# Placed orders by engine, W2 kept in SBUF, and a dense last batch in a block of linear attention and mixture of experts

## The chip, the cores and the metric

One NeuronCore of a Trainium2 chip. TensorE (PE) multiplies matrices, VectorE (DVE), ScalarE (ACT) and GpSimd (POOL) work on tiles, SyncE (SP) issues DMAs; ScalarE and GpSimd issue some too. The time is device microseconds of one execution, lower is better.

## The reference

Eight batches of 1024 tokens, width 128, float32. Each batch goes through attention and then through a mixture of experts, each behind a layer norm that is modulated by the batch's condition vector:

```python
h = _layernorm(x) * (1 + ca) + sa
x = x + ga * attn(h)          # q, k, v, gate = h @ W.T; 8 heads of 16
h = _layernorm(x) * (1 + cb) + sb
x = x + gb * ffn(h)
# attn: rope on q and k; kv = sum_s k v; ksum, vsum
#   o = (q kv / 4 + vsum) / (q ksum / 4 + S) + conv5(v);  return (o * gate) @ Wo.T
# ffn: gates = the two largest of 8 softmax probabilities, scaled to sum 1, else 0
#   y = sum_e gates[:, e] * (gelu(x @ W1[e] + b1[e]) @ W2[e] + b2[e])     # W1 128x256, W2 256x128
```

## The kernel before, in words

A batch is eight blocks of 128 tokens (`J`), handled in two halves of 512 (`CH`). Its attention part, in order: statistics on VectorE (`stat1`), the reciprocal root on GpSimd (`pow1`, L613), the norm on ScalarE (`app1`, L489), transposes to put channels on partitions (`xT`, L337), the q, k, v products of 384 columns a block (`qkv`, L347), rope on VectorE block by block (L777, L779, with the sum of two blocks in L782) and v's eviction on ScalarE (L514), the sums over tokens (`kv`, L360), the transposes of v and q (L354, L368), denominator (`den`, L375), numerator and the spread denominator (`dn`, L381, L386), gate (L391), output product (`out`, L400), the residual (L817), second statistics, `pow2`, `app2`, transposes (`x1T`, L407) and router logits (`logit`, L415).

The sort: VectorE finds the two experts of each token in a chain of small operations (`choose` from L684, `soften`), TensorE counts the ranks (`prefix`, L424 and L426), VectorE makes from them a row number for each token and choice (`put`; `slots`) and the expert of each of 23 tiles of 128 rows (`owner`). GpSimd then scatters the normed rows into `x_sort` in HBM by 16 indirect DMAs of 128 rows (`scat`, L637).

The experts run over the 23 tiles: SyncE reads the tile's expert from `owner` into a register and loads that expert's W1, W2 and b1 as one piece of 514 columns into a ring of eight `wbuf` (`w`, L288 and L289), and four tiles of rows at a time (`xg`). TensorE transposes four tiles (`xsT`, L439), ScalarE evicts them with the modulation (L564), TensorE runs the first layer for couples of tiles (`l1`, L451), ScalarE the gelu (L574), TensorE the second layer (`l2`, L462); ScalarE evicts (`oev`, L582) and issues the store to `o_sort` (`ost`, L590). When all are stored, GpSimd gathers two rows for each token by 16 indirect DMAs (`gat`, L647), VectorE adds them times their gates to the bias product (`comb`, L833 and L836; `b2`, L470), and finishes (`fin`, L842, L845). SyncE stores the output (L303). A float32 product runs as two passes, so it has two records; a transpose has one.

The order on every engine comes from one table: each step has a tick (`AT`), each batch an offset (`BEGIN` for attention and sort, `BEGIN_EXPERTS` for the rest), and all engines walk the steps of all batches in the order of the sum. Attention of batches starts about 162 ticks apart, and the experts of a batch come some 420 to 600 ticks after its first transposes, so the experts of batch b lie beside the attention of batch b + 3, and those of the last three batches beside none. Every engine executes in order, so a wait holds back all that stands behind it. Attention's products share three PSUM banks in turn (`BANKS`). x_sort has four buffers, o_sort two, x1 and the gates are kept for five batches (`LAG`). A batch's first store to `o_sort` waits for the combination of two batches before; its first gather for the batch before (`s_comb`).

## Time and profile before

| | |
|---|---|
| median of 3 runs | 648.53 us (645.81 to 649.82) |
| the profiled execution, first to last instruction | 656.4 us |
| TensorE, weight loads | 453.0 us (69%), 373.7 us (57%) |
| VectorE, ScalarE, GpSimd | 328.3, 298.8, 298.5 us |
| DMA | 107.81 MB, mean 164 GB/s |
| mean granted clock of TensorE | 0.827 |

The profile is one execution under the profiler. Its own time is the span in the second row, and it is about 1% above the runs. Busy times are those of records: a TensorE record says when an instruction was taken up, and its end is modelled. "Issue" or "remote" behind a wait means that no event in the profile explains it.

### The profile page before, as it was taken

The numbers are of one execution on the slowest core, as the hardware profiler recorded it, in microseconds if no ns is written. First come the engines' busy times: TensorE is split into PE (matmuls) and PEld (weight loads), VectorE is DVE, ScalarE is ACT, GpSimd is POOL, SyncE is SP. The second block draws the span as 40 slices with busy tenths as digits, with TensorE's granted clock in tenths as the row PEclk, the third lists the DMA queues.
The fourth block names the chain that finished last, engine by engine and source line by source line (L and its number), as shares of the span: only waits on it lengthen the run. The fifth ranks groups of instructions, "written<-read, shape, count | busy, mean of one in ns | idle before, by whom it ended". The sixth has DMA issues, their size and how long they took to land.

```text
span 656.4 us, 9883 instructions
## 1 busy us (share of the span) xinstructions
PE 453.0 (69%) x2808; PEld 373.7 (57%) x2808; DVE 328.3 (50%) x1070; ACT 298.8 (46%) x805; POOL 298.5 (45%) x293
## 2 busy tenths in 40 slices
PE   2887769699795898587947988398639116693710
PEld 1555439589584876485827976296528115682600
DVE  3678889387372766375743856294127000220242
ACT  1545438478571756265624846173513004361400
POOL 1112463532757275717472557445744760027053
PEclk9987699899987899779875899599955657896765
DMA  7704039688673867277645765566744325975422
GB/s 233 224 1 124 22 107 271 195 233 240 177 218 81 231 199 224 75 220 195 181 133 157 208 183 166 160 186 179 203 137 148 109 73 148 282 213 179 132 64 60
DMA packets 113845, 107.81 MB, mean 164 GB/s; under 512 B 10040, under 2 KB 85440, under 8 KB 113536
## 3 DMA queue, kind: packets, MB, share of 16 engines
q1 hardware_dynamic: 80848, 77.76, 41.8%
q0 software_dynamic: 8192, 16.79, 8.4%
q10 hardware_dynamic: 24752, 12.64, 6.5%
q8 instruction: 23, 0.38, 0.3%
q14 instruction: 30, 0.25, 0.1%
HBM read 76.47 MB, written 30.68 MB: 163 GB/s over the span
## 4 chain that ended last, share of the span: by engine, by line
PE 39%; another core or an unknown queue 23%; DVE 13%; ACT 9%; POOL 6%; issue 6%; DMA 3%; SPq 2%; ACTq 0%; POOLq 0%; DVEq 0%
PE ps_o L462 9%; PE ps_hid L451 9%; PE bank L347 5%; PE bank L360 3%; ACT xn L489 3%; ACT hid L574 2%; PE ps_x L439 2%; DVE stats L658 2%; POOL og L647 2%; POOL x_sort L637 2%; PE ps_z L470 2%; PE bank L415 1%; POOL rstd L613 1%; PE bank L400 1%
## 5 line engine op out<-in xcount | busy, mean ns | idle before, releaser
L637 POOL DMA_INDIRECT x_sort<-xn,slots x128 | 140.6, 1098 | 136.3 <-DVEq L742 100.7
L647 POOL DMA_INDIRECT og<-o_sort,slots x128 | 123.4, 964 | 111.0 <-DMA o_sort<-o_s 46.7
L574 ACT ACTIVATE hid<-ps_hid,wbuf 128x128 f32<-128x128 f32 x368 | 105.1, 377 | 121.3 <-remote 66.5
L462 PE MATMUL ps_o<-wbuf,hid 128*128 128x128 f32 x736 | 111.6, 302 | 65.5 <-issue 41.2
L462 PEld LDWEIGHTS ps_o<-wbuf,hid 128*128 128x128 f32 x736 | 101.1, 212 | 77.5 <-issue 48.2
L451 PE MATMUL ps_hid<-xs_t,wbuf 128*128 128x128 f32 x736 | 111.2, 296 | 14.9 <-issue 11.8
L451 PEld LDWEIGHTS ps_hid<-xs_t,wbuf 128*128 128x128 f32 x736 | 101.5, 210 | 25.1 <-issue 20.1
L833 DVE SCALAR_TENSOR_TENSOR u<-og,gate,ps_z 128x128 f32<-128x128 f32 x64 | 21.9, 343 | 125.4 <-PE ps_z L470 112.2
L613 POOL TENSOR_TENSOR rstd<-var_eps,minus_half 128x8 f32<-128x8 f32 x16 | 27.0, 1688 | 97.1 <-DVE var_eps L668 96.5
L347 PE MATMUL bank<-wqkvg_f,h 128*128 128x384 f32 x128 | 52.3, 531 | 8.9 <-ACT v L514 7.0
L564 ACT ACTIVATE xs_t<-ps_x,mod 128x512 f32<-128x512 f32 (+1 forms) x48 | 37.4, 779 | 24.2 <-PE ps_x L439 13.9
L760 DVE SCALAR_TENSOR_TENSOR conv<-v_t,lepe_f,conv 128x1024 f32<-128x1024 f32 x32 | 40.6, 1269 | 0.2
L777 DVE TENSOR_TENSOR qk_cos<-bank,rope_f 128x256 f32<-128x256 f32 x64 | 26.8, 419 | 27.5 <-PE bank L347 21.0
L582 ACT ACTIVATE o_s<-ps_o 128x512 f32<-128x512 f32 (+1 forms) x48 | 28.4, 592 | 25.8 <-remote 15.3
L347 PEld LDWEIGHTS bank<-wqkvg_f,h 128*128 128x128 f32 x128 | 22.9, 204 | 26.1 <-ACT v L514 14.1
L684 DVE TENSOR_TENSOR logit<-bank,br_f 128x64 f32<-128x64 f32 x8 | 1.8, 222 | 67.3 <-remote 60.8
L439 PE MATMUL ps_x<-consts_f,xg 128*128 128x128 f32 x184 | 30.9, 289 | 6.0 <-DMA xg<-x_sort 4.1
L360 PE MATMUL bank<-v,qk 128*128 128x129 f32 x128 | 22.8, 351 | 16.9 <-DVE logit L684 16.8
L514 ACT ACTIVATE v<-bank 128x128 f32<-128x128 f32 x64 | 16.5, 280 | 35.7 <-DVE qk_sin L779 32.6
L360 PEld LDWEIGHTS bank<-v,qk 128*128 128x128 f32 x128 | 21.8, 264 | 17.7 <-issue 17.5
L489 ACT ACTIVATE xn<-xs,shift,rstd 128x128 f32<-128x128 f32 x64 | 26.2, 507 | 9.7 <-POOL shift L615 9.7
L470 PE MATMUL ps_z<-b_f,gates_t 64*128 64x512 f32 x32 | 19.8, 703 | 14.6 <-issue 11.7
(122 smaller groups left out, 687.2 us busy)
## 6 DMA issues: line engine op xcount, KB each, us to landing
wbuf<-in_w_all SPq DMA_DIRECT2D x184, 257.0 KB
xg<-x_sort SPq DMA_DIRECT2D x40, 256.0 KB
o_sort<-o_s ACTq DMA_DIRECT2D x40, 256.0 KB
x_sort<-zero SPq DMA_DIRECT2D x20, 256.0 KB, 4.5
xs<-in_x SPq DMA_DIRECT2D x8, 512.0 KB
out<-y SPq DMA_DIRECT2D x16, 256.0 KB
x_sort<-xn,slots POOLq DMA_INDIRECT x128
og<-o_sort,slots POOLq DMA_INDIRECT x128
```

What stands on the lines that cost most here:

```text
L347: pe.matmul(of(f"qkv_{j}", b)[:, 0:3 * D], h1[i][:, t], wqkvg_f[:, 0:3 * D], start=True, stop=True)\
L360: last = pe.matmul(of("kv", b)[:, 0:D + 1], qk[:, j, D:2 * D], v[:, j, :], start=(j == 0), stop=(j == J - 1))
L439: last = pe.transpose(ps_x[:, t * P:(t + 1) * P], xg[k % XG_RING][:, t, :], ident)
L451: last = pe.matmul(ps_hid[k % 2][:, m % 2, h, :], wbuf[w % W_RING][:, h * P:(h + 1) * P], xs_t[g % XS_RING][:, t], start=True, stop=True)
L462: last = pe.matmul(ps_o[:, m % GROUP, :], hid[k % HID_RING][:, m % 2, h, :], wbuf[w % W_RING][:, HID + h * D:HID + (h + 1) * D], start=(h ...
L489: last = act.activation(dst[:, j, :], src[:, j, :], ACT.Identity, bias=shift[n][:, j:j + 1], scale=rstd[n][:, j:j + 1])
L564: act.activation(xs_t[k % XS_RING][:, 0:many * P], ps_x[:, 0:many * P], ACT.Identity, bias=mod[:, 3, b:b + 1], scale=mod[:, 4, b:b + 1]).t ...
L574: last = act.activation(hid[k % HID_RING][:, m % 2, h, :], ps_hid[k % 2][:, m % 2, h, :], ACT.Gelu, bias=w[:, 2 * HID + h:2 * HID + h + 1])
L613: pool.tensor_tensor(rstd[n][:, :], var_eps[n][:, :], minus_half[:, :], ALU.pow).then_inc(s_pw[n], 1)
L637: pool.indirect_dma_start(x_sort[b % SORTS], bass.IndirectOffsetOnAxis(ap=at, axis=0), xn2[i][:, n, :], None).then_inc(s_scat[b % SORTS], 16)
L647: pool.indirect_dma_start(og[:, k, n, :], None, o_sort[i], bass.IndirectOffsetOnAxis(ap=at, axis=0)).then_inc(s_gat[n], 16)
L760: dve.scalar_tensor_tensor(conv[:, :], v_t[:, k:k + S], lepe_f[:, k:k + 1], conv[:, :], ALU.mult, ALU.add)\
```

## The change

- The tick table is replaced by one table for each engine, in which each step of each batch has a rank of its own; PSUM banks are given by a table too (`BANK`), four for three, with the bias product among them.
- Batches 0 to 6 are sorted as before. Batch 7 (`DENSE`) is not: its router and gates are computed, then all eight experts for all its tokens, in 16 units of an expert and a half batch (`d1`, `dg`, `d2`, `dc`), and each result is added into `u` times the gate, which is zero for experts that were not chosen. `u` starts from the bias product (`bz`).
- W2 of all experts (1 MB) is loaded once into `w2_f`, and the second layer addresses it by a register that TensorE loads for each tile. `wbuf` now holds W1 and b1 alone (258 columns), has ten pieces, and is free after the gelu. W1 of all experts is also loaded once for the dense batch (`w1_f`).
- q and k of two blocks make one bank of 512 columns, and v of four blocks another; the rope's three operations each cover two blocks.
- `LAG` 6 for 5, three `xn2` for two, three `xs_t` for two, three x_sort for four. Slots and owners have a buffer for each batch.
- Stores to `o_sort` go out from SyncE's queue and wait for the gathers of two batches before; a batch's gather of block n waits for the combination of the same block in the batch before.
- x is loaded in halves, first of all loads; the two halves of the modulation row are read back separately; some scratch lies in buffers that are not yet in use.

```diff
+SORTED = 7
+DENSE = tuple(range(SORTED, B))
+QUAD = 4
...
+    "POOL": {
+        "pow1": [[0], [1], [4], [14], [24], [50], [60], [86]],
+        "wog": [[2]],
+        "pow2": [[3], [13], [23], [33], [53], [71], [87], [120]],
+        "scat": [[5, 6, 7, 8, 9, 10, 11, 12], [15, 16, 17, 18, 19, 20, 21, 22], [25, 26, 27, 28, 29, 30, 31, 32], [42, 43,
+            44, 45, 46, 47, 48, 49], [61, 62, 63, 64, 65, 66, 67, 68], [78, 79, 80, 81, 82, 83, 84, 85], [96, 97, 98, 99,
+            100, 101, 102, 103]],
+        "gat": [[34, 35, 36, 37, 38, 39, 40, 41], [51, 52, 54, 55, 56, 57, 58, 59], [69, 70, 72, 73, 74, 75, 76, 77], [88,
+            89, 90, 91, 92, 93, 94, 95], [104, 105, 106, 107, 108, 109, 110, 111], [112, 113, 114, 115, 116, 117, 118, 119],
+            [121, 122, 123, 124, 125, 126, 127, 128]],
...
+        "d1": [[], [], [], [], [], [], [], [435, 437, 439, 447, 448, 450, 452, 454, 456, 458, 460, 462, 464, 466, 468, 470]],
+        "d2": [[], [], [], [], [], [], [], [438, 440, 442, 449, 451, 453, 455, 457, 459, 461, 463, 465, 467, 469, 471, 472]],
...
+BANKS = 4
...
+        LAG, SORTS, XN2 = 6, 3, 3
+        WCOLS = HID + HH
...
+        W_RING, XG_RING, XS_RING, HID_RING, O_RING = 10, 3, 3, 2, 2
+        w2_f = sb("w2_f", [P, E * HID])
+        w1_f = sb("w1_f", [P, E, WCOLS]) if DENSE else None
         wbuf = [sb(f"wbuf{i}", [P, WCOLS]) for i in range(W_RING)]
...
+                elif kind == "late":
+                    sp.dma_start(w2_f[:, :], w2).then_inc(s_w["late"], 16)
+                    if DENSE:
+                        sp.dma_start(w1_f[:, :, :], w1.rearrange("e p f -> p e f")).then_inc(s_w["late"], 16)
...
+                elif kind == "ost":
+                    k, first, many = quad(b, n), n * QUAD, quad_tiles(n)
+                    if b >= 2 and n == 0:
+                        for j in range(J):
+                            sp.wait_ge(s_gat[j], 16 * TOP * (b - 1))
+                    sp.wait_ge(s_oe, k + 1)
+                    sp.dma_start(o_sort[b % 2][first * P:(first + many) * P, :].rearrange("(t p) d -> p t d", p=P),
+                                 o_s[k % O_RING][:, 0:many, :]).then_inc(s_os[k % O_RING], 16)
...
                     if b == 0 and n == 0:
                         pe.wait_ge(s_w["attn"], 16)
                     if n % 2 == 0:
                         pe.wait_ge(s_h1, CH * b + n // 2 + 1)
-                    for j in (2 * n, 2 * n + 1):
-                        t = slice(j * P, (j + 1) * P)
-                        bank_free(f"qkv_{j}", b)
-                        pe.matmul(of(f"qkv_{j}", b)[:, 0:3 * D], h1[i][:, t], wqkvg_f[:, 0:3 * D], start=True, stop=True)\
-                            .then_inc(s_qkv, 1)
+                    bank_free("qk", b, n)
+                    for j in (0, 1):
+                        t = slice((2 * n + j) * P, (2 * n + j + 1) * P)
+                        last = pe.matmul(of("qk", b, n)[:, j * 2 * D:(j + 1) * 2 * D], h1[i][:, t], wqkvg_f[:, 0:2 * D],
+                                         start=True, stop=True)
+                    last.then_inc(s_qkp, 1)
+                elif kind == "vv":
+                    pe.wait_ge(s_h1, CH * b + n + 1)
+                    bank_free("vv", b, n)
+                    for j in range(JC):
+                        t = slice((n * JC + j) * P, (n * JC + j + 1) * P)
+                        last = pe.matmul(of("vv", b, n)[:, j * D:(j + 1) * D], h1[i][:, t], wqkvg_f[:, 2 * D:3 * D],
+                                         start=True, stop=True)
+                    last.then_inc(s_vv, 1)
                 elif kind == "vT":
...
+                    if n == 0:
+                        pe.wait_ge(s_owner, b + 1)
+                        if b == 0:
+                            pe.wait_ge(s_w["late"], 16 * (1 + bool(DENSE)))
+                    for m in couple_tiles(n):
+                        chosen_w2[b, m] = pe.value_load(owner[b][0:1, m:m + 1], min_val=0, max_val=E - 1)
...
+                        e = chosen_w2.pop((b, m))
...
+                                             w2_f[:, bass.ds(e * HID + h * D, D)], start=(h == 0), stop=(h == HH - 1))
...
+                elif kind == "d1":
+                    e, c = divmod(n, CH)
+                    pe.wait_ge(s_h2, CH * b + c + 1)
+                    if n == 0:
+                        pe.wait_ge(s_w["late"], 2 * 16)
+                    for h, use in enumerate(("d1a", "d1b")):
+                        bank_free(use, b, n)
+                        pe.matmul(of(use, b, n)[:, :], w1_f[:, e, h * P:(h + 1) * P], h2_t[:, c * CT:(c + 1) * CT], start=True,
+                                  stop=True).then_inc(s_d1, 1)
...
+                elif kind == "d2":
+                    e, c = divmod(n, CH)
+                    k = UNITS * DENSE.index(b) + n
+                    pe.wait_ge(s_dg, HH * (k + 1))
+                    bank_free("d2", b, n)
+                    for j in range(JC):
+                        for h in range(HH):
+                            last = pe.matmul(of("d2", b, n)[:, j * D:(j + 1) * D], hid_d[k % 2][:, h, j * P:(j + 1) * P],
+                                             w2_f[:, e * HID + h * D:e * HID + (h + 1) * D], start=(h == 0),
                                              stop=(h == HH - 1))
-                    last.then_inc(s_l2, 1)
...
+                elif kind == "dg":
+                    e, c = divmod(n, CH)
+                    k = UNITS * DENSE.index(b) + n
+                    if n == 0:
+                        act.wait_ge(s_kv, b + 1)
+                        act.wait_ge(s_qT, CH * (b + 1))
+                    if k >= 2:
+                        act.wait_ge(s_d2, k - 1)
+                    for h, use in enumerate(("d1a", "d1b")):
+                        act.wait_ge(s_d1, HH * k + h + 1)
+                        act.activation(hid_d[k % 2][:, h, :], of(use, b, n)[:, :], ACT.Gelu,
+                                       bias=w1_f[:, e, HID + h:HID + h + 1]).then_inc(s_dg, 1)
+                elif kind == "bz":
+                    if n == 0:
+                        act.wait_ge(s_y, CH * b)
+                    act.wait_ge(s_b2, CH * b + n + 1)
+                    act.activation(u[:, n * JC:(n + 1) * JC, :], of("b2", b, n).rearrange("p (j d) -> p j d", d=D), ACT.Copy)\
+                        .then_inc(s_bz, 1)
...
+            def rotate(b, n):
+                src = of("qk", b, n)
+                cos, sin = (rope_f[:, k, 2 * n:2 * n + 2, :].unsqueeze(2).to_broadcast([P, 2, 2, D]) for k in range(2))
+                if b == 0 and n == 0:
+                    dve.wait_ge(s_w["rope"], 16)
+                dve.wait_ge(s_qkp, J // 2 * b + n + 1)
+                if b >= 1 or n >= 2:
+                    dve.wait_ge(s_qk, J // 2 * b + n - 1)
+                dve.tensor_tensor(qk_cos[n % 2][:, :].rearrange("p (j q d) -> p j q d", q=2, d=D),
+                                  src.rearrange("p (j q d) -> p j q d", q=2, d=D), cos, ALU.mult)
+                dve.tensor_tensor(qk_sin[n % 2][:, :].rearrange("p (j q h m) -> p j q h m", q=2, h=2, m=D // 2),
+                                  src.rearrange("p (j q h m) -> p j q h m", q=2, h=2, m=D // 2)[:, :, :, ::-1, :],
+                                  sin.rearrange("p j q (h m) -> p j q h m", h=2), ALU.mult).then_inc(s_rot, 1)
+                if b >= 1 and n == 0:
+                    dve.wait_ge(s_kv, b)
+                    dve.wait_ge(s_qT, CH * b)
+                dve.wait_ge(s_rot, J // 2 * b + n + 1)
+                dve.tensor_tensor(qk[:, 2 * n:2 * n + 2, :].rearrange("p j d -> p (j d)"), qk_cos[n % 2][:, :], qk_sin[n % 2][:, :],
+                                  ALU.add)\
+                    .then_inc(s_qk, 1)
...
+                elif kind == "dc":
+                    e, c = divmod(n, CH)
+                    k = UNITS * DENSE.index(b) + n
+                    if n < CH:
+                        dve.wait_ge(s_soft, SOFT * (b + 1))
+                        dve.wait_ge(s_bz, CH * DENSE.index(b) + c + 1)
+                    else:
+                        dve.wait_ge(s_dc, JC * (k - 1))
+                    dve.wait_ge(s_d2, k + 1)
+                    for j in range(JC):
+                        r = c * JC + j
+                        dve.scalar_tensor_tensor(u[:, r, :], of("d2", b, n)[:, j * D:(j + 1) * D], gates[:, r, e:e + 1], u[:, r, :],
+                                                 ALU.mult, ALU.add).then_inc(s_dc, 1)
```

## Rows read from the trace of the kernel before

**Rows 1.** The page's first two parts: busy times, and the span in 40 slices.

```profile
PE 453.0 (69%) x2808; PEld 373.7 (57%) x2808; DVE 328.3 (50%) x1070; ACT 298.8 (46%) x805; POOL 298.5 (45%) x293
...
PE   2887769699795898587947988398639116693710
...
PEclk9987699899987899779875899599955657896765
```

**Rows 2.** Windows of three stretches: busy us and records by engine, clock, DMA share, GB/s.

```profile
0.00:100.00 100.00, 68.10 (x312) 45.98 (x312) 73.05 (x259) 44.92 (x108) 30.27 (x31) 0.90 0.40 121
100.00:480.00 380.00, 304.15 (x2041) 260.19 (x2041) 215.94 (x700) 209.94 (x571) 202.76 (x194) 0.88 0.65 186
480.00:656.00 176.00, 80.71 (x457) 67.56 (x457) 39.29 (x113) 43.99 (x127) 65.44 (x69) 0.67 0.50 142
```

**Rows 3.** Timeline from 195 to 222 us: of TensorE, VectorE and GpSimd.

```profile
199.87 1.95 PE L415 MATMUL bank<-wr_f,h_t 128*128 128x8 f32 x16 [0.47 <-ACT h_t L548]
...
215.18 3.46 PE L360 MATMUL bank<-v,qk 128*128 128x129 f32 x16 [3.47 <-DVE logit L684]
...
214.80 0.23 DVE L684 TENSOR_TENSOR logit<-bank,br_f 128x64 f32<-128x64 f32 x1 [13.20 <-remote]
...
195.16 0.98 POOL L647 DMA_INDIRECT og<-o_sort,slots  x1 [0.31 <-issue]
...
213.86 0.96 POOL L647 DMA_INDIRECT og<-o_sort,slots  x1 [0.30 <-issue]
```

**Rows 4.** The chain at 358 and 186 us, and TensorE's timeline at 169 us.

```profile
358.82 1.34 PE ps_hid L451 x12
...
186.46 1.29 PE bank L347 x4
...
169.45 1.02 PE L381 MATMUL bank<-q_t,kv_s 128*128 128x512 f32 x2
170.31 0.60 PE L386 MATMUL bank<-consts_f,rden_x 128*128 128x128 f32 x4
```

**Rows 5.** Waits of the whole span: us in total, times, longest.

```profile
DVE logit L684 <- remote: 60.8, 4, 20.5
...
ACT v L514 <- DVE qk_sin L779: 32.6, 31, 7.3
...
PE ps_o L462 <- ACT hid L574: 22.7, 10, 11.7
...
PE bank L347 <- ACT v L514: 7.0, 6, 1.8
```

**Rows 6.** The end: a window at 511 us, and the timeline from 619 to 656 us.

```profile
511.00:545.00 34.00, 2.48 (x12) 1.97 (x10) 0.00 (x0) 2.36 (x8) 22.03 (x23) 0.56 0.29 85
...
621.05 1.60 PE L462 MATMUL ps_o<-wbuf,hid 128*128 128x128 f32 x12 [0.79 <-ACT hid L574]
...
627.26 0.95 POOL L647 DMA_INDIRECT og<-o_sort,slots  x1 [21.07 <-DVE u L836]
...
650.14 0.69 DVE L845 TENSOR_TENSOR y<-u,x 128x512 f32<-128x512 f32 x1
```

**Rows 7.** Groups by line and shape: busy us, mean ns of one, idle before.

```profile
L564 ACT ACTIVATE xs_t<-ps_x,mod 128x512 f32<-128x512 f32 x40 | 32.0, 800 | 16.4 <-PE ps_x L439 13.5 <-remote 2.8
...
L777 DVE TENSOR_TENSOR qk_cos<-bank,rope_f 128x256 f32<-128x256 f32 x64 | 26.8, 419 | 27.5 <-PE bank L347 21.0 <-remote 5.9 <-issue 0.5
...
L782 DVE TENSOR_TENSOR qk<-qk_cos,qk_sin 128x512 f32<-128x512 f32 x32 | 22.3, 698 | 1.1
L833 DVE SCALAR_TENSOR_TENSOR u<-og,gate,ps_z 128x128 f32<-128x128 f32 x64 | 21.9, 343 | 125.4 <-PE ps_z L470 112.2 <-DMA og<-o_sort,slots 13.2
```

**Rows 8.** SyncE's register load, its arithmetic and an address: ns least, median, most.

```profile
L288 SPq TENSOR_LOAD <-owner x184: 3/268/1053, 87.4 to 612.4; - x184
L288 SPq FUSED_REGOPS  x184: 3/152/700, 87.9 to 612.7; - x184
...
L289 SPq FUSED_REGOPS  x184: 3/37/700, 88.2 to 613.0; - x184
```

854 lines of the change are left out of this document (465 added, 389 removed), and 72 rows, old and new, of tables (AT, BANK).

## The prediction

> **What bounds the kernel now.** The page comes first, for shares: TensorE is busy 453.0 us of a span of 656.4 us, in 2808 matmul records, and no other engine passes 50% [rows 1]. So TensorE is nearest to a bound, but a third of the span is not its work. The slices say where: they are full from about 80 to 480 us and half empty after it, and the granted clock falls there too [rows 1]. The windows give it in numbers [rows 2]: TensorE has 304.15 us busy of 380 in the middle, and 80.71 of 176 after 480 us, at a mean clock of 0.67.
>
> Busy time hides two things, a low clock and a stalled engine, so I count in records at the full clock instead. A 128 column record takes 1.34 / 12 = 0.112 us, a 384 column one 1.29 / 4 = 0.323, a 512 column one 0.86 / 2 = 0.43 (from the start of one row to that of the next) [rows 4]. By the code 128 records have 384 columns (q, k and v of eight blocks in eight batches, two passes), 96 have 512 (num, gate and the bias product), and 2584 have about 128. That is 41.3 + 41.3 + 289.4 = 372 us of work, 0.1325 us a record. In the middle 2041 records make 270 us in 380: TensorE runs at 0.71 of what it could. After 480 us 457 records make 61 us in 176.
>
> What is the rest of the middle? The timeline at 195 to 220 us shows it [rows 3]. TensorE's record of the logit products lies at 199.87 to 201.8, but VectorE's first operation on them starts at 214.80, 13.20 us late, and the kv products of TensorE 0.4 us behind that. In all this time GpSimd issues gathers at an even 1.25 us, and VectorE starts when the last of them, at 213.86, ends. The waits name four such pauses in front of the logit line alone, 60.8 us [rows 5]. I read this as a pause that a long run of indirect DMAs on GpSimd brings with it, and that a change which keeps those runs keeps too. After 480 us the same happens with less to cover it: from 511 to 545 us TensorE is busy 2.48 us of 34, and GpSimd 22.03. The end is a chain of one batch: last expert products at 621.05, gathers from 627.26, last output operation at 650.14 [rows 6].
>
> A rule of the Trainium skill speaks against this reading: "SBUF — State Buffer", section "SBUF: two separate sides", has only VectorE and GpSimd sharing a port, and TensorE and ScalarE waiting on nobody. By it the 13.20 us are no price of the gathers, and a better placed order could win them back; that is the first rival below, whose time comes from the rows.
>
> **The change, part by part.** The sum is made against the profiled span of 656.4 us; the median of the runs is 648.53, 7.9 us less, and I take 8 us off at the end.
>
> 1. Batch 7 is not sorted. Gone are 207 records of 128 columns (23 tiles: one transpose, four passes in each layer) and 9 of the prefix sums: 216 x 0.112 = 24.2 us of TensorE. Gone are 16 scatters and 16 gathers at 1.25 us, 40 us of GpSimd, and their chain at the end [rows 3, 6].
> 2. Batch 7 is computed by all eight experts: 16 units (expert, half). The first layer has 4 records of 512 columns a unit, 64 x 0.43 = 27.5 us; the second 16 of 128, 256 x 0.112 = 28.7 us. Together 56.2 us. Beside a unit's 3.5 us of TensorE lie two gelus of 512 columns, at some 0.80 us (xs_t's evictions of that width), and four accumulations of 0.343 us [rows 7]: 1.6 and 1.4 us, so TensorE bounds these units if its clock is full. The lone buffer for the second layer's result is read in 1.4 us while the next first layer runs 1.7 us; that cover is thin, and I take 0.9 of full speed. In the order table 13 of the 16 units stand behind the last sorted expert: 45.7 us, 51 at 0.9. Behind the last are 1.4 us of accumulation and what the last output operation of before takes to the end, 656.4 - 650.1 = 6.3 us [rows 6]: 8 us.
> 3. The wide q, k and v: the rope's twelve operations a batch are all 512 wide at 0.698 us, 8.4 us, where 26.8 us of 64 cosine products, as much for sine and 22.3 for the sums made 9.5 us a batch [rows 7]. VectorE has half its time free, so 1 us a batch counts nothing. q, k, v in 256 and 128 columns make 41.8 us of TensorE for 41.3. A v eviction no longer waits inside the rope: 32.6 us of ScalarE's waits, 7.0 of TensorE's [rows 5]. I count the 7.
> 4. W2 stays in SBUF and w1 comes in pieces of half the size, released after the gelu. 23 x 7 pieces of about 129 KB instead of 184 of 257 KB are 27 MB less. No wait of TensorE on these loads is among the long ones, and the DMA share in the middle is 0.65 [rows 2], so this hides and counts nothing; were the loads late, it would be a gain.
> 5. The price of that: TensorE loads a register for each tile, 161 times, behind the first layer of its couple, and addresses the second layer by it. On SyncE the same load took 0.268 us with 0.152 us of register work, and an address 0.037 [rows 8]. A couple has two loads, 0.84 us, and some 0.15 to 0.3 us of addresses. Ahead of them stand 8 records, 0.9 us, which the array can still work on while the sequencer loads, if its queue holds them. In 84 couples that is 0 at the least and 84 x 1.1 = 92 us at the most; a gain is excluded, since before these are plain addresses. The records ahead are as long as the loads, which puts it near the lower end: I take 12 us.
> 6. Orders: placed by engine, with four banks for three, XN2 of 3, x1 for 6 batches, W_RING 10. Batch 7's attention is spread over the experts of batches 4 to 6, where before the last three batches' experts stood alone. This is what fills the part after 480 us. In the middle it can shorten waits such as 22.7 us of the second layer for the gelu [rows 5]; against it, o_sort's stores move from ScalarE's queue to SyncE's, where a store that waits for an eviction holds back the w1, xg and x loads behind it, and the experts wait for those. Bounds: 22.7 us won, 20 us lost; I take 10 won.
> 7. GpSimd: 224 indirect DMAs for 256. The table places 16 in a row, and gathers straight behind scatters, where now twelve and four stand apart. I take the pause for each set as it is.
> 8. The start: no wait for the modulation before the first transposes, x loaded first; 5 us won at most, left out, since 2 MB of w2 and w1 are queued there as well.
>
> **The sum.** The new total is 372 - 24.2 + 56.2 + 0.5 = 404.5 us. The first 100 us do 312 records [rows 2], 41 us, as now. 45.7 us are the dense tail. Between lie 317.8 us, at 0.71: 447.6 us. So 100 + 447.6 + 51 + 8 = 606.6; minus 7 (3), minus 10 (6), plus 12 (5): 602. In the unprofiled measure 594 us.
>
> **Rivals.**
> - The pauses are the order's, not GpSimd's. Without the 60.8 us of pauses the middle does 270 in 319, 0.85; 317.8 / 0.85 = 374 us, and the end is at 528, 520 unprofiled; with half of them, 559. For it: the port rule, and that the pauses sit where VectorE's fixed order waits. Against: the even gathers, and that the pause ends with them.
> - The pauses grow. At 511 to 545 us TensorE misses 31.5 us in one run [rows 6], where the four of the middle have 60.8 / 4 = 15.2 each. The table sets gathers directly against scatters three times: 3 x 16.3 = 49 us, 643. Half clock in the dense tail would cost 45.7 / 0.5 - 51 = 40 us, 634. For it: the clock of 0.67 after 480 us; against: TensorE has more work queued in both places.
> - TensorE's register loads are exposed (the slower side). The sequencer stands 0.84 us in loads and 0.25 in addresses per couple with little queued, 84 x 1.1 = 92 us in place of my 12: 674 us. It decides from (655 - 594 + 12) / 84 = 0.87 us a couple. For it: the load is as long as the records that cover it, and the waits ahead of it (the next layer's weights) empty the queue. Against: records queue ahead of the array elsewhere.
> - The change does not do what it says: the dense batch fills nothing. Its second layer norm is placed on GpSimd behind the 16 gathers of batch 5, and the first unit needs h2. If those gathers wait for batch 5's last stores, TensorE waits for 20 us of them, their pause of 13 and the norm, transposes and evictions of some 10: 594 + 43 = 637.
>
> **How the numbers follow.** Forecast (575 to 620) 0.42; smaller pauses (515 to 575) 0.22; longer pauses or half clock 0.13 and a late dense batch 0.08 (620 to 643); register loads exposed 0.13, of this 0.01 within 1%; neither gain nor loss of note for reasons I do not see 0.02. A measurement here can tell about 1%, 642 to 655, and the first of the slow cases reach into it with 0.02. Faster 0.83, same 0.05, slower 0.12. The range leaves out a tenth at each end: 540 from within the first rival, 655 where the exposed loads begin to decide.
>
> **What would show it.** Right: 112 gathers and 112 scatters; windows with TensorE above 0.85 busy until some 60 us before the end; in the last 50 us 512 column records at 0.43 us; pauses of 5 to 14 us in VectorE still ending with GpSimd's runs; TensorE's register loads at 0.27 us with gaps below 0.2 us behind them. Wrong: gaps of a microsecond between the layers of each couple; dense units at 7 us; a middle without pauses beside the same GpSimd runs, which would free far more than I forecast.

## The result: slower by 9%, and where the time lies in the profile after

The changed kernel takes 708.5 us (median of six runs, 701.7 to 708.7), the kernel before 649.2 us (644.5 to 661.0): a ratio of 1.092, with an interval of 1.086 to 1.097. I had predicted 594. The sum behind that number was 602 us for a profiled execution. This one has a span of 702.6, 101 us more. The page's head, under [rows 1] of before:

```profile
PE 507.8 (72%) x3040; PEld 419.7 (60%) x3040; DVE 333.9 (48%) x1036; ACT 298.5 (42%) x733; POOL 256.9 (37%) x261
...
PE   5296869679851948976897679585749839934996
...
PEclk9799778879975876989798779757759958985999
```

The last third is filled, as planned. But the middle, which was nearly full before, now has holes. Windows of the profile after (columns as in [rows 2]) say how deep:

```profile
200.00:300.00 100.00, 70.78 (x442) 60.59 (x442) 42.70 (x134) 44.42 (x113) 46.27 (x49) 0.77 0.40 111
...
400.00:500.00 100.00, 71.35 (x394) 60.53 (x395) 42.81 (x128) 41.13 (x107) 42.66 (x44) 0.73 0.38 109
```

Before, 380 us of the middle held 2041 records [rows 2], 5.4 a microsecond; these 200 us hold 836, 4.2. The pause that I had read at 201 us of the kernel before [rows 3] is there again, in front of the same logit line. VectorE's timeline has the first operation behind it, GpSimd's the last gather:

```profile
229.75 0.23 DVE L876 TENSOR_TENSOR logit<-bank,br_f 128x64 f32<-128x64 f32 x1 [30.60 <-PE bank L561]
```

```profile
220.62 0.94 POOL L836 DMA_INDIRECT og<-o_sort,slots  x1 [0.30 <-issue]
```

VectorE stands for 30.6 us where it stood for 13.2, and the 8 us behind the last gather are new: TensorE's products, which it waits for by the releaser, come late as well.

I split the missing 101 us in two. The last first-layer products of the sorted experts start at 601.5 us, their second layer ends at 606. Up to 601.5 I had 100 + 447.6 - 7 - 10 + 12 = 542.6, so the start and middle are 59 us late. Behind it I had 51 + 8 = 59 and find 101: the tail is 42 us too long. A part of these 42 is only a wrong border. I had put 13 of the 16 dense units behind the last sorted product. In the table all 16 are there (their ranks are 435 to 472, the last sorted one is 433), and so they are in the trace. Three units, 10.5 us of work, belong to the tail and not to the middle; the middle is later, and the tail less too long, by 10 to 15 us. The tail in windows, and in the chain:

```profile
606.00:620.00 14.00, 13.03 (x81) 10.03 (x81) 7.69 (x29) 6.29 (x11) 6.15 (x7) 1.00 0.24 69
620.00:640.00 20.00, 3.26 (x6) 0.80 (x4) 4.24 (x11) 0.27 (x1) 9.07 (x10) 0.64 0.14 39
640.00:654.00 14.00, 9.89 (x13) 3.53 (x14) 6.88 (x22) 3.23 (x5) 0.00 (x0) 0.55 0.11 33
654.00:695.00 41.00, 40.99 (x242) 30.11 (x241) 12.61 (x45) 15.84 (x24) 0.00 (x0) 1.00 0.00 1
```

```profile
654.11 1.78 PE bank L638 x16
655.89 1.72 PE bank L629 x4
```

From 654 us on, the dense units run as forecast: 1.78 + 1.72 = 3.5 us each, at full clock. Twelve of the sixteen are done so. The other four, 14 us of work, lie in the 52.5 us before, beside some 10 us of other products. TensorE and ScalarE stand there for one thing, by their timelines:

```profile
637.54 2.04 PE L582 MATMUL bank<-b_f,gates_t 64*128 64x512 f32 x2 [14.09 <-DVE u L1037]
```

```profile
644.63 0.60 ACT L782 ACTIVATE u<-bank 128x512 f32<-128x512 f32 x1 [22.43 <-PE bank L582]
```

The bias product of the dense batch waits for a bank and `bz` waits for `s_y`, both until batch 6 has been gathered and added up, since the two batches share `u`. Batch 6's 16 gathers run from 612 to 632 us, with a pause in them.

For the pauses I use one count throughout. It is the length, within 2 us before to 3 us behind each run of GpSimd's indirect DMAs, of all stretches of at least 1.5 us in which TensorE's weight loads, VectorE and ScalarE together start no more than two instructions in a microsecond. It gives 161 us for the kernel before and 135 us for the one after, which has two sets of DMAs fewer. So over the whole span the pauses have become shorter, not longer. This count is coarse. Taken again over the same traces (windows of 1 us moved by 0.1 us, instructions of the sequencers included, a row ends where no DMA follows within 2 us), it gives 161 and 140 us. I call this the second count; it agrees with the first within 5 us where both were made. Either takes ordinary waits beside GpSimd's DMAs for pauses too.

### The profile page after: what moved, and what is told of

Read it like the earlier page. It is cut to its first block, busy times and chain, and to the rows that moved or that the text cites. A ratio compares the mean times of both kernels' runs of the same rounds, so it can differ in the third digit from the quotient of the medians.

```text
span 702.6 us, 11067 instructions
## 1 busy us (share of the span) xinstructions
PE 507.8 (72%) x3040; PEld 419.7 (60%) x3040; DVE 333.9 (48%) x1036; ACT 298.5 (42%) x733; POOL 256.9 (37%) x261
## 4 chain that ended last, share of the span: by engine, by line
PE 49%; another core or an unknown queue 23%; issue 9%; DVE 9%; ACT 8%; DMA 2%; SPq 0%; ACTq 0%; DVEq 0%
PE ps_hid L602 10%; PE ps_o L619 9%; PE bank L629 4%; ACT hid L757 3%; PE bank L638 3%; PE bank L481 3%; PE bank L582 2%; PE bank L517 2%; PE bank L537 2%; PE bank L524 2%; PE bank L561 2%; PE ps_x L590 2%; PE bank L503 1%; DVE qk_cos L952 1%
## 5 line engine op out<-in xcount | busy, mean ns | idle before, releaser
L826 POOL DMA_INDIRECT x_sort<-xn,slots x112 | 115.1, 1028 | 107.7 <-DVE slots L937 75.7
L619 PE MATMUL ps_o<-w_f,hid 128*128 x644 | 105.1, 315 | 47.1 <-issue 19.2
L619 PEld LDWEIGHTS ps_o<-w_f,hid 128*128 128x128 f32 x644 | 94.4, 224 | 57.6 <-issue 57.1
L952 DVE TENSOR_TENSOR qk_cos<-bank,rope_f 128x512 f32<-128x512 f32 x32 | 21.9, 683 | 44.6 <-PE bank L481 23.6
L481 PE MATMUL bank<-wqkvg_f,h 128*128 128x256 f32 x128 | 40.1, 447 | 1.6 <-issue 1.4
L582 PE MATMUL bank<-b_f,gates_t 64*128 64x512 f32 x32 | 22.6, 792 | 21.4 <-DVE u L1037 17.0
L638 PEld LDWEIGHTS bank<-w_f,qk 128*128 128x128 f32 x256 | 30.7, 192 | 7.1 <-issue 6.0
L489 PE MATMUL bank<-wqkvg_f,h 128*128 128x128 f32 x128 | 20.4, 308 | 19.3 <-DVE qk_sin L954 10.9
L776 ACT ACTIVATE qk<-bank,w_f 128x512 f32<-128x512 f32 x32 | 21.9, 687 | 29.2 <-PE bank L629 26.6
L629 PE MATMUL bank<-h_t,w_f 128*128 128x512 f32 x64 | 32.4, 635 | 0.8 <-ACT u L782 0.8
```

What stands on the lines that cost most here:

```text
L481: last = pe.matmul(of("qk", b, n)[:, j * 2 * D:(j + 1) * 2 * D], h1[i][:, t], wqkvg_f[:, 0:2 * D], start=True, stop=True)
L582: pe.matmul(of("b2", b, n)[:, :], gates_t[b % LAG][:, :], b2_f[:, n * CT:(n + 1) * CT], start=True, stop=True)\
L619: last = pe.matmul(ps_o[:, m % QUAD, :], hid[k % HID_RING][:, m % 2, h, :], w2_f[:, bass.ds(e * HID + h * D, D)], start=(h == 0), stop=(h ...
L629: pe.matmul(of(use, b, n)[:, :], w1_f[:, e, h * P:(h + 1) * P], h2_t[:, c * CT:(c + 1) * CT], start=True, stop=True).then_inc(s_d1, 1)
L638: last = pe.matmul(of("d2", b, n)[:, j * D:(j + 1) * D], hid_d[k % 2][:, h, j * P:(j + 1) * P], w2_f[:, e * HID + h * D:e * HID + (h + 1) ...
L826: pool.indirect_dma_start(x_sort[b % SORTS], bass.IndirectOffsetOnAxis(ap=at, axis=0), xn2[b % XN2][:, n, :], None).then_inc(s_scat[b % SO ...
```

## The experiments

**The machine has two conditions, and each comparison lies within one.** On some occasions the kernel before took 656 to 666 us, near the 649 of the first. On others it took 492, with few pauses: the second count gives 4 to 32 us for e1, e2, e3, e13 and e14 (the kernel before itself has no trace there). One and the same chip showed 492 us and, an hour later, 664. I call them "with pauses" and "without". A ratio is always to the kernel before on the same chip in the same stretch of time. "Placed" is the change's order, "old" the tick table. The runs with pauses come from three chips (e5 to e8, e9 to e12, and e17 with e18), so between these groups only ratios can be set side by side. Beside e5 to e8 the kernel before spread from 638 to 664 us; these four ratios are the roughest.

| run | order | W2 | us | ratio (95%) |
|---|---|---|---|---|
| **with pauses** | | | | |
| e5 changed kernel | placed | register | 704.9 | 1.082 (1.068 to 1.095) |
| e6 | placed, own sum | constants | 692.1 | 1.059 (1.048 to 1.070) |
| e12 | placed, own sum | register | 709.9 | 1.066 (1.056 to 1.076) |
| e18 broken rows | placed, own sum | register | 654.0 | 0.986 (0.981 to 0.991) |
| e7 | old, own sum | register | 665.0 | 1.014 (of the medians; runs spread over 26 us) |
| e9 | old, own sum | constants | 669.4 | 1.008 (1.004 to 1.012) |
| e10 | old, own sum | ring | 676.4 | 1.016 (1.008 to 1.024) |
| e11 stores on ScalarE's queue | old, own sum | ring | 673.2 | 1.013 (1.008 to 1.018) |
| e8 batch 7 sorted | old | register | 693.9 | 1.051 (1.034 to 1.069) |
| e17 wide rope in before | old | ring | 670.9 | 1.013 (1.008 to 1.018) |
| **without** | | | | |
| e1 | placed | constants | 518.9 | 1.053 (1.046 to 1.060) |
| e3 = e12 | placed, own sum | register | 515.5 | 1.046 (1.041 to 1.051) |
| e16 = e18 | placed, own sum | register | 571.8 | 1.160 (1.149 to 1.170) |
| e2 before with loads | old | ring | 500.7 | 1.013 (1.007 to 1.019) |
| e4 before, plain DMAs | old | ring | 483.6 | 0.980 (0.971 to 0.989) |
| e13 = e17 | old | ring | 491.6 | 0.998 (0.994 to 1.003) |
| e14 dense batch in before | old, own sum | ring | 498.1 | 1.012 (1.004 to 1.020) |
| e15 broken rows in before | old | ring | 562.5 | 1.145 (1.135 to 1.154) |

### Register loads

```diff
# e1 (and e6, e9): the choice of W2 by the tile's expert is left out
-                        chosen_w2[b, m] = pe.value_load(owner[b][0:1, m:m + 1], min_val=0, max_val=E - 1)
...
-                        e = chosen_w2.pop((b, m))
+                        e = m % E
# e2: the kernel before, behind each l1
+                    for m in couple_tiles(n):
+                        pe.value_load(owner[b][0:1, m:m + 1], min_val=0, max_val=E - 1)
```

> The changed kernel without TensorE's register loads: the second layer addresses W2 by a constant, tile number modulo 8, so it leaves out the choice of W2 (its output is not the reference's). Theory A, TensorE's register loads are what makes it slow: a tile's load takes 0.30 + 0.15 us and gaps, about 1.3 us a couple in 84 couples, so 40 to 90 us come back, 620 to 665 us. Theory B, the time is lost in the pauses of the indirect DMAs and in the order: at most 10 us come back, 698 or more. Theory C, the shared accumulator of the tail: no change here either.

> The kernel before with one thing added: TensorE loads each tile's expert into a register behind the first layer, as in the changed kernel, and does not use it (owner has eight buffers so that nothing is overwritten). Theory A: 40 to 90 us slower, 690 to 740. Theory B and C: within 10 us of 649.

Without pauses, 184 added loads cost 6.2 us (1.3%), so 161 would cost 5.4. The sequencer's rows in the profile after, with least, median and most in ns:

```profile
L610 PEldq TENSOR_LOAD <-owner x161: 293/300/752, 111.9 to 601.8; - x161
L610 PEldq FUSED_REGOPS  x161: 146/151/165, 112.5 to 602.2; - x161
L619 PEldq FUSED_REGOPS  x322: 46/46/51, 118.0 to 605.0; - x161
```

A tile has 0.30 + 0.15 + 2 x 0.05 = 0.54 us of sequencer time, 88 us in all, and nearly all of it lies beside work of the array.

### The accumulator of the dense batch

```diff
# e3: and the dense units have banks 1, 2, 0; b2 of batch 7 comes before them, comb of batch 6 between them
+        u_d = h1[0][:, :].rearrange("p (j d) -> p j d", d=D)
...
-                        act.wait_ge(s_y, CH * b)
+                        act.wait_ge(s_gate, CH * b)
```

> The changed kernel with an accumulator of its own for the dense batch (in a buffer that is free by then), the dense batch's bias product ahead of unit 1, fixed banks for the dense units, and batch 6's combination between dense units on VectorE. Theory C: the dense units no longer wait for batch 6's gathers, so they run from 608 us of the span at 3.5 us each and end near 665: 30 us come back, 678. Theories A and B leave the middle as it is, so no more than that; if the pause of batch 6's gathers holds TensorE all the same, 15 us come back, 693.

> The placed orders with register loads and an accumulator of its own for the dense batch, once more, as the fourth corner beside the three in the old order. If the placed orders lose by themselves, this is 1.045 to 1.075, 20 to 30 us above the kernel in the old order with the same registers (1.014); if they lose only together with the registers, the earlier run with placed orders and constants (1.059) would have to come down to the run with constants and the old order, which it then does not.

With pauses it is 1.066 after 1.082, from two chips, with touching intervals, some 10 us by the medians. The tails in the traces show less. From the end of the last sorted second layer to the end of the span they take 96.7 us (first trace of the changed kernel) and 92.6 us (e5), and with an accumulator of its own 93.0 us (e12) and 89.8 us (e6). On one chip, e5 against e6, that is 3 us. Without pauses the tail of e3 still takes 84.7 us. So most of its length is neither the shared accumulator nor a pause. Without pauses I have no run of the unaltered change beside e3, so the gain can't be told there.

### Without indirect DMAs

```diff
# e4: the kernel before; which row goes where is left out (gathers alike)
-                        pool.indirect_dma_start(x_sort[b % SORTS], bass.IndirectOffsetOnAxis(ap=at, axis=0), xn2[i][:, n, :],
-                                                None).then_inc(s_scat[b % SORTS], 16)
+                        pool.dma_start(x_sort[b % SORTS][(k * J + n) * P:(k * J + n + 1) * P, :],
+                                       xn2[i][:, n, :]).then_inc(s_scat[b % SORTS], 16)
```

> The kernel before with each indirect DMA of GpSimd replaced by a plain one of the same size and count, issued by GpSimd at the same place: rows go in order, so it leaves out the sort (its output is not the reference's). If the pauses come from the indirect DMAs themselves, the four pauses in front of the logit line (60.8 us) go and the time falls by 50 to 100 us, to 550 to 600. If they come from any DMA that GpSimd issues, or from the order, nothing falls: 640 to 655.

It fell into the condition without pauses and gives 2% there (an interval of 1 to 3%). What plain DMAs would do where the pauses are wasn't measured.

### The changed kernel itself, and both repairs

> The changed kernel unaltered, so that the variants can be set against it on one chip. If its loss against the kernel before belongs to the kernel and not to the chip on which it was first timed, the ratio is 1.09 again: 536 us where the kernel before takes 492. If half of the loss came from longer pauses beside GpSimd's indirect DMAs, it shrinks to 1.03 to 1.06 on a chip that hardly has them. The two single repairs gave 1.053 (W2 chosen by constants) and 1.046 (an accumulator of its own for the dense batch), so I expect 1.08 and that each repair is worth 3% of the time.

> Both repairs together: the dense batch has an accumulator of its own (and its bias product early), and TensorE takes W2 by constants in place of registers; the choice of W2 by the tile's expert is left out. If register loads (about 14 us) and the shared accumulator (about 18 us) are separate costs, they add up: 1.08 less 0.027 less 0.034, 1.02, 502 us beside 492. If both remove the same wait, it stays at 1.04. What is left above 1.00 then lies with the placed orders and with the stores on SyncE's queue, since TensorE's own work is 32 us more and would explain 1.02 to 1.03 by itself.

The ratio stands. Both repairs together win 12.8 us of 49, less than I had expected: the main cause is elsewhere.

### Old order, dense batch or not

All steps of the change walk in the order of the tick table again. The dense units stand behind it at 12 ticks each:

```diff
# e7; e8 besides has SORTED = 8 and no accumulator of its own
-        k = BANK[use][b][n]
+        k = 3 if use == "b2" else TURN[0] % 3
+        TURN[0] += use != "b2"
...
-    for _, kind, b, n in sorted(ranks):
+    for kind, b, n in RANKS[engine]:        # from TICK, BEGIN and BEGIN_EXPERTS of the kernel before
         stage(kind, b, n)
```

> Undoes the placed orders alone: all steps of the changed kernel (W2 resident with registers, wide rope, dense last batch with its own accumulator) walk in the order of the old tick table, with three banks in turn and one for the bias product; the dense units stand behind the last sorted products, 12 ticks apart. Compare with the changed kernel with its own accumulator, 1.046. If the placed orders cost time, this is under 1.03; if they win time by filling the last third (my step 6, 10 us won), it is 1.06 to 1.09; if the order does not matter, 1.045.

> As the one before, but batch 7 is sorted like the others, so that only the resident W2 with its registers, the wide rope, the buffers and SyncE's stores remain of the change. TensorE has 32 us less work than with the dense batch. If the dense batch is what costs, this is at 1.01 to 1.02, the price of the register loads (1.0125 when added to the kernel before); if the wide rope and the smaller loads give something, below 1.01; if the stores on SyncE's queue hold back the weights, 1.03 or more.

The placed orders lose: the old order with the same instructions is at 1.014, the placed one at 1.066 (the edit takes back the orders of all engines and the sequence of the banks together). The dense batch wins: 665.0 against 693.9 us with it sorted. The windows of 400 to 500 us, of the old order (first) and the placed one:

```profile
400.00:500.00 100.00, 77.10 (x512) 67.71 (x513) 53.06 (x147) 49.20 (x129) 52.17 (x49) 0.86 0.43 121
```

```profile
400.00:500.00 100.00, 64.61 (x391) 54.96 (x390) 47.76 (x143) 37.74 (x98) 49.23 (x50) 0.78 0.38 110
```

GpSimd does as much in both (52 and 49 us); TensorE does 121 records less. The pauses add up to 98 us in the old order and 146 us in the placed one: 48 us, where the spans differ by 47 (663.5 and 710.9). These two traces are from different chips. On one chip, e9 has the old order and e12 the placed one, and they differ besides in the register loads. There the second count gives 109 and 144 us, 35 us, and the spans differ by 36 (674.9 and 710.9).

Both have 224 indirect DMAs, but in different rows. In e12 twelve rows have 16 DMAs and the others 4 or 8. In e7 the first four have 12 and 4, and from 169 us on there are five of 14, four of 16 and two of 18, with short ones between. By the second count the rows of 16 and 18 have 11.6 us of pause each on the average, in e12 as in e7, and the rows of 14 in e7 have 3.3. The placed order has twelve long rows where the old one has six.

### Registers, ring and queue in the old order

```diff
# e10: W2 with W1 in a ring of eight again; e11 also has the ost stage on ScalarE
+                        w = wbuf[tile(b, m) % W_RING]
...
-                                             w2_f[:, bass.ds(e * HID + h * D, D)], start=(h == 0), stop=(h == HH - 1))
+                                             w[:, HID + h * D:HID + (h + 1) * D], start=(h == 0), stop=(h == HH - 1))
```

> The changed kernel in the old order, with its own dense accumulator, and W2 chosen by constants, so that TensorE loads no register and computes no address; the choice of W2 by the tile's expert is left out. Its pair with the register loads took 665 us beside 656 (1.014) on a chip with long pauses. Register loads exposed: 84 couples by up to 0.4 us, 0.96 to 0.98 here. If the loads lie beside other work, as my prediction had it (12 us or less, 2%), 0.995 to 1.01.

> The same in the old order, but W2 comes with W1 in the ring of eight pieces as in the kernel before, for the sorted tiles; the computation is whole. If only TensorE's register loads cost, this equals the run with constants, 0.96 to 0.98, and is a version that beats both kernels. If the larger loads had cost something before, it is 0.01 or more above that run.

> As the ring version in the old order, with the stores to o_sort issued from ScalarE's queue again, as before. What is left of the change is the dense last batch, the wide rope and the buffers. If the stores on SyncE's queue hold back the weights and rows behind them, this is 0.01 to 0.03 faster than the ring version; if they hide, the same. Against the kernel before: 0.94 to 0.98, since the dense batch takes some 27 us of chain off the end.

All four (e7 is the run with registers) lie between 1.008 and 1.016. I had expected 0.94 to 0.98 of e11, and was wrong. Neither the register loads nor the pieces' size nor the queue of the stores makes a difference that I can measure. The fourth corner, e12, was timed beside these three: 709.9 against 669 to 676 us. The placed orders' loss is 5%.

### The wide rope, and the dense batch alone

```diff
# e13, e17: the kernel before
-USES = {"qkv": lambda n: [f"qkv_{2 * n}", f"qkv_{2 * n + 1}"],
+USES = {"qkv": lambda n: [f"qk_{n}"] + ([f"vv_{n // 2}"] if n % 2 else []),
# e14: e11 with the 384 column products, the rope by blocks and v's evictions of the kernel before
-                    bank_free("qk", b, n)
+                    for j in (2 * n, 2 * n + 1):
+                        bank_free("qk", b, j)
```

> The kernel before with the wide q, k and v alone: q and k of two blocks in one bank, v of four blocks in another, the rope's three operations 512 wide. If the 4% that remain unexplained belong to this part, the ratio is 1.03 to 1.05. If they belong to the buffers and waits (three x_sort for four, gathers released block by block), it is 0.99 to 1.01, as my prediction had it.

> The wide q, k and v alone in the kernel before; 0.998 on a chip where the kernel before takes 492 us. Where it takes 655, the changed kernel in the old order with all batches sorted is at 1.051, with 0.6% of it for register loads. If the wide rope makes the rest, 1.03 to 1.05; if it does not, 0.99 to 1.01, and the rest lies with the three x_sort buffers, the three banks' new sequence or the waits added.

> The other way round: changed kernel in the old order, W1 and W2 in one ring, stores from ScalarE's queue, q, k and v in 384 columns and the rope block by block again, so that in essence only the dense last batch (with its own accumulator) is left of the change. Its pair with the wide rope took 1.013. If the wide rope costs 4%, 0.97; if the buffers do, 1.01.

The wide rope costs 1.3% with pauses and nothing without. It doesn't explain the 5.1% of e8. With the loads at 1% or less, some 3% stay with the buffers, the added waits and the bank sequence; no run tells these apart. Alone, without pauses, the dense batch doesn't pay (1.012), but its 32 us more of TensorE's work show as only 5.5 us of time.

### Broken rows

```diff
+            def breath():
+                for k in (next(breaths), next(breaths), next(breaths)):
+                    pool.tensor_tensor(spare[:, k * J:(k + 1) * J], ones[:, :], ones[:, :], ALU.pow)
...
+                    if n == JC:        # in scat and in gat: between the eighth and the ninth DMA
+                        breath()
```

> The kernel before with three small operations of GpSimd, some 5 us, between the eighth and the ninth DMA of each set of scatters and of gathers; they compute nothing that is used. If the pauses come from the length of an uninterrupted row, their sum of 161 us falls to under 100 and the ratio is 0.93 to 0.97 on a chip with long pauses. If each DMA has its own price, the pauses stay and the 5 us show at the end: 1.00 to 1.03.

> The same break in the changed kernel with its own dense accumulator and the placed orders (1.066 beside this chip's kernel before). If the placed orders lose because they set 16 DMAs in a row, 1.00 to 1.03; if they lose for another reason (their waits on each other when the execution doesn't keep the planned times), 1.06 to 1.09.

> Placed orders with own accumulator and each row of 16 DMAs broken in two by some 5 us of small operations. On a chip without pauses the break costs 11% (571.8 against about 515 us), which is 14 breaks of 4 us on GpSimd's chain. Where the kernel before takes 655 us: if long rows make the pauses, their sum of 146 us falls below 90 and the time to below 1.04 of the kernel before in spite of the breaks' own cost; if not, the sum stays above 120 and the ratio is 1.08 or more.

Two windows of one set of gathers in e12, rows unbroken, from 204.9 to 224.7 us:

```profile
205.00:216.00 11.00, 6.33 (x51) 5.82 (x50) 0.00 (x0) 5.55 (x17) 8.52 (x9) 0.96 0.50 136
216.00:228.00 12.00, 0.00 (x0) 0.00 (x0) 0.00 (x0) 0.18 (x1) 6.61 (x7) 0.51 0.44 121
```

In these 12 us, in which the last seven DMAs lie, TensorE and VectorE do nothing, ScalarE one operation. In e18 the second half of that set comes after the break, and is worked through by all engines:

```profile
221.00:232.00 11.00, 9.64 (x55) 8.90 (x55) 7.75 (x27) 2.43 (x9) 7.89 (x8) 0.80 0.35 94
```

```profile
247.03 4.89 POOL L803 TENSOR_TENSOR spare<-ones 128x8 f32<-128x8 f32 x3
```

The second fence is GpSimd's timeline at the next break, in the set behind: 4.89 us of work that nobody needs. Fourteen such breaks bring the pauses from 146 to 94 us, and the time from 709.9 to 654.0 us (against each one's kernel before, from 1.066 to 0.986). I had expected less than 90 us of pauses if the rows make them and over 120 if not; 94 is just outside the first, and far from the second. Within e18 the length of a row decides too: of 19 rows of eight, 18 have pauses of 5 us or less, while four places where halves of two sets follow each other, 16 in a row again, have 10.8, 6.4, 14.2 and 13.8 us. In the first two of these 2.5 and 4.0 us lie between the halves, which is not enough to bring the pauses down to those of two rows of eight; in the last two nothing does. Where there are no pauses, the same edit does what one expects of 4.9 us on a busy engine. It costs 56 us (e16 against e3), and in the kernel before 70 us (e15), where the chain now belongs to GpSimd. Neither expectation was met; that of e15 was written for a chip with pauses. What the break does in the kernel before, or in the old order, with pauses wasn't measured. The chain of e15:

```profile
POOL 55%; issue 14%; PE 13%; DVE 8%; ACT 4%; DMA 4%; POOLq 0%; ACTq 0%; DVEq 0%
```

The next table sets the traces side by side. TensorE's work is that of the sum, at full clock; the pauses are the second count's; the rest is what is left of the span.

| trace | span | TensorE's work | pauses | rest |
|---|---|---|---|---|
| kernel before | 656.4 | 372 | 161 | 123 |
| changed kernel | 702.6 | 404.5 | 140 | 158 |
| e12 placed | 710.9 | 404.5 | 144 | 162 |
| e7 old order | 663.5 | 404.5 | 99 | 160 |
| e9 old order, constants | 674.9 | 404.5 | 109 | 161 |
| e18 placed, broken rows | 659.6 | 404.5 | 92 | 163 |
| e3 = e12, without pauses | 515.1 | 404.5 | 8 | 103 |

It shows two things. Among e12, e7, e9 and e18 the rest is the same within 3 us: what the placed order loses to the old one, and what the breaks win, lies in the pauses. The change's 46 us against the kernel before do not lie there. Of them 32 are work, the pauses are 21 us less, and 35 are rest, which the old order has as well. No run tells what this rest is made of. The granted clock is a part of it, 0.80 from 100 to 600 us where the kernel before had 0.88 from 100 to 480. That rows of 16 make longer pauses in this condition is shown by e18. Whether the number of DMAs in a row counts, the time they take or what is still under way isn't. The length alone doesn't do it either: without pauses, e3 has a row of 48 and 8 us of pauses in all.

## Why the prediction was wrong, point by point

**The step that failed is the seventh: "I take the pause for each set as it is".** I had named that the table sets 16 in a row where 12 and 4 stood apart, but in the sum priced the pauses by the middle's efficiency of 0.71, as if a pause were a fixed price of a set. It depends on how long a row runs unbroken. The placed orders therefore lose 36 us of span to the old order on one chip (47 between two), with 35 (48) us more of pauses, and a break in each row takes the loss away. From 100 to 600 us the profile after has 2314 records, 0.1325 x 2314 = 307 us of work in 500, an efficiency of 0.61 where I had kept 0.71. At 0.71 they would have taken 432 us, so 68 us are lost there.

Of these 68 the pauses are less than half. By the second count the middle before had 80 us of pauses beside 172 DMAs, 0.47 us for each, and the 500 us here have 118 beside 192, 0.62; the old order (e7) has 92 beside 201, 0.46, as before. At 0.47 it would be 89, so longer pauses make 29 us. The other 39 lie outside the counted pauses, in the rest of the table above, and their cause stays open. That 0.71 also stood for the clock and the waits of the middle before, and that the change would keep those, was the other half of this step. The reading that the pauses go with GpSimd's runs was right.

**The sixth step** took 10 us won from the placed orders. With rows of 16 it lost: 36 us on one chip. With the rows broken the placed order stands at 0.986, below the old one's 1.008 to 1.016, so the order may be worth something apart from its rows; the old order with broken rows, which would show it, wasn't run. Without pauses the order that was placed keeps TensorE nearly full. Here is the same kernel (own sum, placed) from 100 to 400 us, without pauses and with them:

```profile
100.00:400.00 300.00, 288.08 (x2142) 256.64 (x2143) 212.51 (x656) 212.86 (x554) 200.96 (x198) 0.97 0.64 177
```

```profile
100.00:400.00 300.00, 221.50 (x1439) 194.96 (x1440) 154.63 (x499) 147.28 (x376) 131.61 (x132) 0.84 0.40 113
```

My 0.1325 us a record makes 284 us of 300 in the first, 0.95, and 191 us, 0.64, in the second.

**The first and second steps, work and tail.** The dense unit is right, 3.5 us, and so are the 8 us behind the last: the last product ends at 694.7 us, the kernel at 702.6. What is missing in the sum is the wait ahead of them. I wrote down that `u` starts from the bias product, but not that batch 6 holds `u` until its gathers are added up, and a pause of 15 us fell on the same place. The term of 51 us should have been 93; of the difference 10.5 us are the three units that I had put into the middle. The own accumulator brought back only 3 us of it in the traces, and without pauses the tail is still 84.7 us long. Still, the dense batch is worth 29 us with pauses. That this is because it takes the last set and its pause off the end (in e8, as in the kernel before, the last scatters and gathers make one row of 32 with over 30 us of pause) fits the traces but is argued; for TensorE it is 32 us more work.

**The third step** hid the rope and won 7 us; with pauses it costs 1.3%, without them nothing. **The fourth** (W2 resident counts nothing) and **the queue of the stores** hold. **The fifth** took 12 us for the register loads, where e2 gives 5.4 without pauses, and e7 and e9 differ by 0.6% with them: the slower side that I had named did not come. **The eighth** holds: the first 100 us do 335 records for 312.

**The rivals.** "The pauses grow" named the mechanism, but I gave it 16.3 us more at the three places where gathers follow scatters, 49 us, and 643 us in total. In the trace after, no row has more than 16 DMAs, so this didn't happen. What did was twelve rows of 16, 11 us of pause each, where the kernel before has seven of 16 or 18 and its one row of 32. "The dense batch fills nothing" foresaw a late tail for the wrong wait: x1 and the second norm came in time, and the shared sum did not. "The pauses are the order's" put the time without them at 520 us, and the variants of the change take 515 to 519 us there. That is luck, since the kernel before takes 492 then, so the change isn't faster either. TensorE has 372 us of work in one and 404.5 in the other, but this isn't the 23 us between them: e14 has the same dense work in the old order and takes 5.5 us more. Of the other 17 the register loads are 5.4; orders, buffers and stores have the rest, which no run divides. **The port rule of the Trainium skill** ("SBUF — State Buffer", section "SBUF: two separate sides") would let TensorE and ScalarE run beside GpSimd. The windows of e12 show both stopped for 12 us beside seven DMAs, so the rule doesn't bound what an indirect DMA can do to them. It is about ports, and what stops them here need not be a port. I was right not to lean on it, and wrong to think I had seen the whole price of the pauses.

## What to carry to other kernels

A stall that goes with another engine's activity has a shape as well as a size: see where in the run of that activity it begins before you count it per set, and ask of every reordering whether it makes such runs longer. Before a dense or fused tail is costed by its units, follow its first input and its accumulator back to who frees them. And time a schedule in both conditions of the machine if there are two: here the same break wins 8% in one and costs 11% in the other. Last, when a loss is put down to one cause, set work, that cause and the rest beside each other in every trace; here it showed that the cause of the order's loss was not that of the whole change's.

## What the runs showed of the hardware that I had not expected

The same kernel (e3 and e12) takes 515 or 710 us, with the same data. Beside GpSimd's rows single instructions take longer with pauses, even such as touch no memory at all: SyncE's register arithmetic behind its load, least, median and most in ns, without pauses and with them:

```profile
L397 SPq FUSED_REGOPS  x161: 152/152/181, 76.6 to 416.2; - x161
```

```profile
L397 SPq FUSED_REGOPS  x161: 3/152/812, 77.5 to 604.0; - x161
```

In the kernel before the most is 700 ns [rows 8]. With pauses ten of the 161 take over 200 ns. All ten stand within a row of indirect DMAs or at most 1.1 us behind it, and only four of them within 2 us of a counted pause. A delay of instructions that read registers alone speaks for something that all the sequencers share, such as the way by which instructions reach them, and against the SBUF ports. That is argued, not shown: no run here changed the number of instructions or their place alone. One look at the traces speaks against its plainest form. The queue that the page calls instruction moves as much in both, first without pauses, then with them, and one of its transfers takes 0.97 and 1.05 us at the median:

```profile
q8 instruction: 28, 0.46, 0.4%
```

```profile
q8 instruction: 28, 0.46, 0.3%
```

Nor did any run show what puts the machine into one condition or the other; the chip doesn't decide it, since one chip showed both (492 and 664 us for the kernel before).

In e12's twelve rows of 16 the first pause begins 3 to 17 us into the row, in nine of them before 9 us, and in eleven the last one outlasts the row by 1.7 to 3 us (the count looks no further). How short a break would do wasn't tried; the two places in e18 say that 2.5 to 4 us are too little. A version that beats the kernel before was found for one condition only: e18, by 1.4% with pauses (interval 0.9 to 1.9%), and 16% slower without.
